# Reordering ScalarE's factor scaling and GpSimd's weight differences in the head of a two-layer convolution kernel

## The reference, cut to what matters

```python
def _L0_conv_ref(x, g_pos, g_neg, bias, input_factor, output_factor):
    v = dac(x * input_factor)          # round(clip(x, -1, 1) * 127) / 127 * 0.6
    v = jnp.swapaxes(v, -2, -1)
    v = jnp.pad(v, ((0, 0), (0, 0), (PAD, PAD), (PAD, PAD)))
    patches = unfold2d(v, KH, KW, SH, SW)
    fv = patches + CUBIC * patches ** 3
    g = g_pos - g_neg
    outs = [jnp.einsum('bctfyx,ocyx->btfo', fv, g[i]) for i in range(WP - 1)]
    ...
x = x + _L0_conv_ref(_gn(x), ...)
x = x + _L1_conv_ref(_gn(x), ...)
```

## Time and profile before

| | us |
|---|---|
| median of 3 runs (range) | 1580.29 (1579.73 to 1582.46) |
| the profiled execution's own time | 1580.08 |
| its span in the trace | 1578.3 |
| PE busy in the span | 1458.8 (92%) |
| DVE busy | 1390.4 (88%) |
| ACT busy | 1158.5 (73%) |
| POOL busy | 505.2 (32%) |

### The profile page before, as it was taken

The page is one execution under the profiler, slowest core; times in us unless marked ns, Lnnn a source line. Parts: engine busy times, 40 slices in busy tenths (PEclk is TensorE's granted clock), DMA queues, the critical chain, the costliest instruction groups (busy, mean ns, idle before and its releaser), DMA issues.

```text
span 1578.3 us, 22713 instructions
## 1 busy us (share of the span) xinstructions
PE 1458.8 (92%) x7792; PEld 623.7 (40%) x7792; DVE 1390.4 (88%) x2172; ACT 1158.5 (73%) x1505; POOL 505.2 (32%) x506
## 2 busy tenths in 40 slices
PE   1499999999999999999999999999999999999865
PEld 1254434344443444344344433434343444434322
DVE  4769899998989899998989998898999999898646
ACT  4457778786878878787877887787787868776443
POOL 3121333232433333332332423234242424333212
PEclk9799999999999999999999999999999999999987
DMA  5010011313222131323113141321313132212231
GB/s 201 1 54 22 33 28 46 115 28 107 54 77 61 51 107 28 107 54 107 45 40 104 32 116 43 107 54 39 96 40 108 41 107 54 54 27 54 54 80 54
DMA packets 29174, 103.82 MB, mean 66 GB/s; under 512 B 4032, under 2 KB 4224, under 8 KB 29056
## 3 DMA queue, kind: packets, MB, share of 16 engines
q1 hardware_dynamic: 20416, 70.86, 12.2%
q0 software_dynamic: 8640, 31.46, 10.5%
HBM read 37.29 MB, written 33.55 MB: 45 GB/s over the span
## 4 chain that ended last, share of the span: by engine, by line
PE 74%; DVE 18%; issue 4%; ACT 2%; POOL 1%; DMA 1%; SPq 0%; DVEq 0%; POOLq 0%; ACTq 0%
PE A L482 13%; PE A L484 12%; PE A L483 12%; PE L L542 7%; PE B L482 7%; PE B L484 7%; PE B L483 7%; PE L L586 4%; PE L L573 3%; DVE uall L1126 1%; DVE duo L1044 1%; DVE q L1016 1%; DVE A L1096 1%; DVE duo L1093 1%; DVE uall L1099 1%
## 5 line engine op out<-in xcount | busy, mean ns | idle before, releaser
L482 PE MATMUL A<-T,WH 128*128 128x504 f16 (+1 forms) x1152 | 439.8, 382 | 1.0 <-ACT uall L762 1.0
L483 PE MATMUL A<-T,WH 128*128 128x504 f16 (+1 forms) x1152 | 438.2, 380 | 0.0
L484 PE MATMUL A<-T,WL 128*128 128x504 f16 (+1 forms) x1152 | 438.1, 380 | 0.0
L1363 POOL TENSOR_TENSOR T<-t,T 128x512 f16<-128x512 f32 x192 | 244.5, 1298 | 405.1 <-ACT T L695 405.1
L738 ACT ACTIVATE junk<-xr,shift 128x1024 f16<-128x1024 f32 x248 | 284.7, 1148 | 12.0 <-DVE xr L1129 5.2
L1337 POOL TENSOR_TENSOR zl<-z,zh 128x512 f16<-128x512 f32 x120 | 150.8, 1276 | 397.7 <-ACT zh L795 396.8
L482 PE MATMUL B<-T,WH 128*128 128x504 f16 (+1 forms) x576 | 221.6, 385 | 23.6 <-POOL T L1363 14.0
L484 PE MATMUL B<-T,WL 128*128 128x504 f16 (+1 forms) x576 | 220.9, 383 | 0.9 <-issue 0.9
L483 PE MATMUL B<-T,WH 128*128 128x504 f16 (+1 forms) x576 | 220.9, 383 | 0.0
L482 PEld LDWEIGHTS A<-T,WH 128*128 128x128 f16 x1152 | 115.2, 100 | 195.4 <-issue 83.0
L484 PEld LDWEIGHTS A<-T,WL 128*128 128x128 f16 x1152 | 112.8, 98 | 136.5 <-issue 0.7
(11 more groups left out here) (163 smaller groups left out, 2462.1 us busy)
## 6 DMA issues: line engine op xcount, KB each, us to landing
xr<-in_x_dram SPq DMA_DIRECT2D x64, 512.0 KB, 5.8
out_dram<-xr SPq DMA_DIRECT2D x64, 512.0 KB, 2.7
xr<-shared POOLq DMA_DIRECT2D x60, 512.0 KB, 4.6
xr<-in_L_conv_g_pos_dram SPq DMA_DIRECT2D x3, 576.0 KB, 9.7
xr<-in_L_conv_g_neg_dram SPq DMA_DIRECT2D x3, 576.0 KB, 12.0
xr<-in_L_conv_Wm_dram SPq DMA_DIRECT2D x2, 32.0 KB, 9.2
xr<-in_L_conv_Wq_dram SPq DMA_DIRECT2D x1, 32.0 KB, 11.4
xr<-in_L_conv_Wk_dram SPq DMA_DIRECT2D x1, 32.0 KB, 11.1
```

The lines of the kernel that those rows point to most:

```text
L482: nc.tensor.matmul(to, wh, th, start=fresh and y == 1, stop=False, skip_group_check=True)
L483: nc.tensor.matmul(to, wh, tl, start=False, stop=False, skip_group_check=True)
L484: done = nc.tensor.matmul(to, wl, th, start=False, stop=y == 2, skip_group_check=True)
L1363: last = nc.gpsimd.tensor_tensor(low, t32[:, pair, :, :, :].rearrange("p t e w -> p (t e w)"), high, ALU.subtract)
```

## The change

Three edits. ScalarE's scaling of `inf` and its wait for the three factors go behind the statistics of quarters 0 and 2. On GpSimd the second weight difference goes ahead of `scale_x`, and the third goes between the two calls of `rows_low`. SP waits, ahead of the loads of image 1, for the four partial statistics that VectorE takes of image 0 (`head_stats`).

```diff
@@ SP, ahead of the loads of image 1
             sp.dma_start(wm_in[:, IC:P], Wm).then_inc(small_loaded, 16)
+            sp.wait_ge(head_stats, NG)
             for g in range(NG):
                 sp.wait_ge(stats_in[0], g + 1)
                 load(1, 1, g)
@@ ACT, head
             nc.scalar.preload_act_table_set("natural_log_exp_and_others")
-            act.wait_ge(factors_loaded, 16 * 3)
-            nc.scalar.activation(inf[:, :], inf[:, :], ACT.Identity, scale=LEVELS).then_inc(factor_scaled, 1)
             act.wait_ge(consts_made, 1)
             head_stats_x(0)
             head_stats_x(2)
+            act.wait_ge(factors_loaded, 16 * 3)
+            nc.scalar.activation(inf[:, :], inf[:, :], ACT.Identity, scale=LEVELS).then_inc(factor_scaled, 1)
             first_scaled()
@@ POOL, head
             weight_difference(0)
+            weight_difference(1)
             scale_x(0)
-            weight_difference(1)
+            rows_low(0, 0, 0)
             weight_difference(2)
-            rows_low(0, 0, 0)
             rows_low(0, 0, 1)
             phases(pool, phase)
```

## The result

The changed kernel takes 1572.93 us (median of 6 runs, 1571.31 to 1573.81) where the kernel before takes 1580.79 (median of 6, 1577.02 to 1582.74, among them the three runs of the table above): a ratio of 0.995, 95% interval 0.9939 to 0.9961. The profiled execution took 1572.13, its span is 1570.1. (One run of a kernel further down took 2193.72 us at a mean granted clock of 0.656 and counts in no number here.)

A forecast was written before the change was run, and what follows sets the result against it. The prediction took the head's cross-engine chain before the first convolution matmul as the bound: weights turning 6.4 us earlier, less 2.3 for the third difference, rounded to 4.0, gives 1576.3 us against the median of 1580.29; range 1573.8 to 1578.8.

The forecast's parts named there:

- The chain: Head, across engines: a head shorter by d ends the kernel earlier by d; first convolution matmul from 54.06 to about 50.0.
- The removed wait gives nothing by itself: ScalarE's factor scaling moved behind the statistics: only makes everything ready early, with the variance there by 13.1 to 14.8.
- The second difference's start: GpSimd, ahead of the scale: starts 18.2 to 18.8 once its planes land; first level at 23.5, 2.9 us earlier.
- The freed clip and sums: VectorE between first level and weight turn: clip loses 1.06, third sum 2.41; weights turn from 26.3, 6.4 us earlier.
- The third difference: GpSimd between the low rows: shuts out the second transform's opening subtraction, costing 2.3 us on the chain.
- The rival in which it shuts nobody out: Second transform's subtraction passes the third difference: the 2.3 us cost goes, gain 6.3, time 1574.0; chance 0.08.
- The sum: At the first convolution matmul: 6.4 - 2.3 = 4.1, rounded down to 4.0 us earlier.
- against the median of 1580.29: Base of the forecast: the kernel before's median, from which the gain of 4.0 us gives 1576.3 us.
- Nothing behind 54 us hangs on the clock of the wall: After the head: work depends only on earlier instructions, so the head's gain should reach the end in full.
- the rival on TensorE's clock: Head's slow stretches: one longer by up to 3 us loses 1.5, giving 1577.8, or 1574.8 the other way; chance 0.20.
- The slower side: Head: scale waits for late second planes; slower by 0.2% if they land from 22.0 on; chance 0.03.
- the loads: Head's DMA queue: image 1's earlier loads delay the second planes; 2 us of delay give 1578.3; chance 0.10.

The follow-up runs named there:

- the second, whose factors landed early: Profile from repeating the kernel before with no edit: 1580.09 us (12 runs), ratio 1.0002; first convolution matmul at 52.70.
- the two later series: The changed kernel again with no edit, twice: 1574.73 us (10 runs), ratio 0.9968, and on another chip 1575.11 us (12 runs), ratio 0.9978.
- the repeat: The changed kernel run again with no edit, first repeat: 1574.73 us (10 runs), ratio 0.9968 to the kernel before.

## Why the prediction was right and wrong

*The chain.* For the changed kernel right, step by step: the variance was there at about 15.95, and the scale, behind the second difference, began at 20.79. What it says of the parts is wrong. "The removed wait gives nothing by itself" holds only with GpSimd's new order behind it: with the old order it brings the first level to 17.18 and the matmul to 47.38, 6.7 us earlier than before and so more than all edits together. The prediction credits the second difference's new place with an earlier level; that place holds the level back, from about 17 to 22.75. VectorE's small instruction beside the first difference was held (2.56 us), as allowed for.

*The second difference's start.* Forecast 18.2 to 18.8, with the end at 21.4 and the level at 23.5; measured 17.62, held by VectorE's second sum as said (3.07 us for 2.61), end 20.7, level 22.75. Of the missing 0.75 us, some 0.5 are the landing, 17.5 instead of 18.03; the rest are a shorter hold (0.46 us instead of 0.6) and a shorter scale. In five profiles of this order the second difference started between 16.93 and 17.62, in four of other kernels, that with GpSimd's order alone among them, at 17.79 to 18.48: the landing moves by 1.5 us between executions, and one profile gives one draw of it. The scale took 1.96 us, where 2.1 was taken.

So the first term of the sum, 2.9 us at the level, measured 26.43 - 22.75 = 3.7.

*The freed clip and sums.* 2.77 us from level to weight turn (25.52 - 22.75), forecast 2.76.

*The third difference.* Forecast 2.3 us, measured 3.52 - 1.23 = 2.29, and its removal gave it back. The rival in which it shuts nobody out is refuted.

*The sum.* Forecast 4.0 at the first matmul, measured 5.04, 5.45 and 6.25 in three profiles of the change against the first of before. Against the second, whose factors landed early, it is 1.4 less each time, and 4.9 between the means. The runs say 4.4 to 5 us, so the forecast's gain was about 0.4 to 1.0 too small, most of it in the term at the level.

*The numbers, which is where it failed.* The mechanism held; sizes did not, in two further steps. The first is "against the median of 1580.29": three runs, all on the upper side of a kernel whose executions fall into two sorts 4 us apart. The mean of 74 more is 1579.0; taken from there, the forecast of 4.0 would have said 1575.0, and the change's mean is 1574.0. The second is "Nothing behind 54 us hangs on the clock of the wall" and, with it, the rival on TensorE's clock. That the clock can add or take, and that this is luck of a run, was right; the size was not. I priced it at 1.5 us, from a stretch that might be longer "by as much as 3 us", a length that no row gave, and only for the two slow stretches of the head. The end of the program I left out, though the trace of before has it (granted clock third from the end):

```profile
1500.00:1540.00 40.00, 25.21 (x137) 9.42 (x134) 18.71 (x24) 19.62 (x25) 4.84 (x5) 0.82 0.31 79
1540.00:1578.00 38.00, 21.01 (x154) 8.30 (x154) 24.64 (x40) 14.27 (x20) 10.39 (x11) 0.77 0.14 56
```

TensorE is busy for 46.22 of these 78 us, and its clock falls more than once (it is 0.50 from 1520 to 1528 and again from 1536 to 1556). There it is worth 3.4 us, and the range lacked it. Of the 3.4 us between forecast and result, 1.3 are the base, about 1.0 the gain (5.0 over all runs), and the other 1.1 the first series' draw (1572.9 against a mean of 1574.0). That the result lies outside the range is in part such a draw: the medians of the two later series, 1574.73 and 1575.11, lie inside it.

*The slower side and the loads.* Neither came; issuing image 1's loads later left the planes where they were.

What stays open: why the execution's clock takes one course or the other at the end. The runs show the two, and that both kernels have both, by the mean clock of their runs; of the kernel before no profile caught the faster end, and no run here steers it.

## What to carry to other kernels

When a shift in the head is to be worth its full size at the end, follow one instruction through the phases in both traces, and stop where the distance changes: here it moved by 0.6 us at most in 1,350 and by 3.4 in the last 170, where the clock did. Read the granted clock at both ends of the program, and the clock of every timed run, before taking a median as the base. And when two edits are made together, cost each without the other: the wait taken off ScalarE's statistics carried the gain (6.7 us at the first matmul by itself, 5.0 with the rest), and moving a weight difference ahead of the scale put a new wait for a DMA in its place.

## What the runs showed of the hardware that was not expected

- The wait for the other engine goes both ways. GpSimd's difference took 3.07 us where it takes 2.61 when it started 0.17 us behind VectorE's two-input sum (17.62 against 17.45), and VectorE's next sum took 2.92 where it takes 0.54.
- A VectorE instruction on four elements was held as long as a large one: L1001, begun 0.07 us behind the first difference, took 2.56 us, where it took 0.23 in the repeat, in which it ran ahead of the difference. It has one tensor input. The Trainium skill, page "SBUF — State Buffer", section "Who interferes with whom", names instructions with two SBUF inputs or in a two-port mode as those that contend with GpSimd, and `tensor_scalar` as one that can enter such a mode. The trace agrees that one tensor input is no protection; whether this one ran in such a mode no run here shows.
- The landing of the same small load differed by 1.35 us between two executions of the kernel before (ScalarE starts on it at 13.95 and 15.30), and the chain behind it moved as much.
